# Key norms of a random-feature attention computed by two-column products and applied as the bias of the exponential

## The chip, the cores and the metric

The kernel runs on one core of a Trainium2 chip. The metric is the device time of one execution, in microseconds (us); lower is better. The kernel before took 1992.07 us in the median of three runs (1990.9 to 1998.57).

## The reference, cut to what matters

The program is two layers of a graph network on 625 nodes with 768 channels: normalisation, a graph convolution and an attention side by side, then a feed-forward part (the second one a mixture of experts). The change touches only the second layer's attention. It has 12 heads of 64 channels and 256 random features, and is linear in the number of nodes:

```
def _phi(t, random_features):
    norm_sq = 0.5 * jnp.sum(t * t, axis=-1, keepdims=True)
    proj = jnp.einsum('bhnd,md->bhnm', t, random_features)
    return jnp.exp(proj - norm_sq) * (1.0 / math.sqrt(M))
q_p = _phi(q, random_features)
k_p = _phi(k, random_features)
kv = jnp.einsum('bhnm,bhnd->bhmd', k_p, v)
out = jnp.einsum('bhnm,bhmd->bhnd', q_p, kv)
k_sum = jnp.sum(k_p, axis=2)
normalizer = jnp.einsum('bhnm,bhm->bhn', q_p, k_sum)[..., None]
out = out / (normalizer + 1e-06)
```

So each key row of each head needs one number, half the sum of its squares, which is subtracted from 256 projections before the exponential.

## The kernel before, in words

Every operand of a product is held as a high part (fp32r) and a low part (the rest), and a product is two or three matmuls of such parts. A high part is written by ScalarE (`ACT`), the low part by VectorE (`DVE`) as a difference.

The attention is the function `phase_attend`, which is used twice; the second time with `second` true, between 1000 and 1172 us of the profiled execution. After the values it runs over six pairs of heads (`for p in range(PAIRS)`). Each engine has its own queue, written out by hand, and they meet by semaphores. On TensorE one pair is:

- `features_k(p)`: five key tiles of up to 128 nodes. For each tile two products with 512 columns put minus half the squared norm into all 512 columns of a PSUM bank (line 407: the weights are the squares `sq`, the moving operand is `nh`, which holds -0.5 in the rows of one head and 0 in those of the other), and four products with 256 columns add the projections of the two heads (line 411). The banks are 6 and 7 by turns. Between the tiles stand units of the next pair's projection to queries and keys (`project_unit`, six products each, line 191).
- `features_q(p)`: four query tiles (two heads by two halves of the features) of eight products with 314 columns (lines 437 and 445), with a unit of projection after each of the first three.
- `keys_values(p)`: 40 products with 130 columns (line 464), then three more units of projection.
- `attend(p)`: 24 products (line 191) that give numerators and denominators of both heads.

On ScalarE each key tile is two exponentials of all 512 columns from PSUM: line 580 writes the full value to the scratch `pf`, line 581 the high part to `phik`. Then come the next pair's keys (`qk_high`, line 532), the query tiles with two exponentials each (lines 597 and 598) and, after the first of them, the squares of the next keys (`squares`, lines 544 and 545), a piece of the weight ring (`ring_high`, line 128), the high part of the key-value matrix (lines 609 and 613), the next pair's queries, the denominators (line 626), and the squares of the next queries. The second squares go to `sqf`, from which GpSimd makes the low part of the squares (line 346).

On VectorE each key tile is the low part (line 721). After each of the first four key tiles stands the reciprocal of a quarter of the previous pair's denominators (line 729). Then come the next keys' low part (line 681), `normalise(p - 1)` (line 690, numerators times reciprocals), the low parts of the four query tiles (line 742), a piece of the weight ring (line 139), the key-value matrix (lines 759, 762 and 767), the next queries' low part and a copy of the numerators (line 783). The scratch `pf` has two buffers, so an exponential waits for the low part two tiles earlier.

Of the kernel before, what the change touches and what calls it, by code (L numbers as in the profile page):

```python
# [258 lines left out]
def phase_attend(k, name, second, rf=None):  # L259
# [3 lines left out]
    with ExitStack() as ctx:  # L263
# [15 lines left out]
        if second:  # L279
            scratch = k.x[:].rearrange("p t d -> p (t d)")  # L280
            pf = scratch[:, 0:2 * NT].rearrange("p (a n) -> p a n", a=2)
            sqf = scratch[:, 2 * NT:4 * NT].rearrange("p (a n) -> p a n", a=2)
            den = scratch[:, 4 * NT:5 * NT]
            sq = k.sb(f"{name}_sq", [P, 2, 2, NT], F32R)
            nh = k.sb(f"{name}_nh", [P, 512], F32R)
            tiny = k.sb(f"{name}_tiny", [P, 1], F32)
            k.x_dram = k.nc.dram_tensor("x_dram", (NODES, D), F32).ap()
        else:
            bv, bq, bp = k.v_bias, k.qk_bias, k.out_bias
        s = signals(k, name, (  # L290
            "saved", "rf_in", "chain", "ones_set", "rf_turned", "rf_bd", "rf_hi", "rf_ready", "v_mm", "v_f", "v_hi",
            "v_lo", "qk_mm", "qk_hi", "qk_lo", "sq_hi", "sq_lo", "pk_mm", "pk_f", "pk_hi", "pk_lo",
            "pq_mm", "pq_f", "pq_hi", "pq_lo", "kv_mm", "kv_part", "kv_f", "kv_hi", "kv_lo", "at_mm", "den_f", "num_f",
            "at_out"))
# [8 lines left out]
        def qk_count(p, a):  # L303
            return 2 * p + (1 if a == KEYS else 2)

        def key_bank(t):
            return k.banks[6 + t % 2][0:TS[t], 0:512]

        def query_pair(m):
            return k.pair[0] if m % 2 == 0 else k.pair[3]  # L310
# [43 lines left out]
        def _(pe):  # L354
# [20 lines left out]
            def project_unit(p, u):  # L375
# [13 lines left out]
                if j == KD - 1:  # L389
                    mm.then_inc(s["qk_mm"], 1)  # L390

            def features_k(p):
                pe.wait_ge(s["qk_lo"], qk_count(p, KEYS))
                for t in range(TT):
                    i = p * TT + t
                    if i >= 2:
                        pe.wait_ge(s["pk_hi"] if second else s["pk_lo"], i - 1)
                    if t < 2 and p >= 1:
                        pe.wait_ge(s["pq_hi"] if second else s["pq_lo"], 4 * p)
                        if second:  # L400
                            pe.wait_ge(s["den_f"], 2 * p - 1)
                            pe.wait_ge(s["num_f"], 2 * p - 1)
                    if second:
                        if t == 0:
                            pe.wait_ge(s["sq_lo"], qk_count(p, KEYS))
                        for a in range(2):
                            pe.matmul(key_bank(t), sq[:, KEYS, a, t * P:t * P + TS[t]], nh[:], start=(a == 0), stop=False)
                    for hd in range(2):
                        out = key_bank(t)[:, hd * MF:(hd + 1) * MF]
                        for a in range(2):  # L410
                            mm = pe.matmul(out, qk[:, KEYS, hd, t * P:t * P + TS[t]], rf2[:, a, :],
                                           start=(a == 0 and not second), stop=(a == 1 and (hd == 1 or not second)))
                    mm.then_inc(s["pk_mm"], 1)
                    project_unit(p + 1, t)
                project_unit(p + 1, TT)
# [91 lines left out]
        def _(act):  # L507
# [61 lines left out]
            for p in range(PAIRS):  # L569
                for t in range(TT):  # L570
                    i = p * TT + t
                    act.wait_ge(s["pk_mm"], i + 1)
                    if p >= 1 and t == 0:
                        act.wait_ge(s["kv_mm"], p)
                    if second:
                        if t >= 2:
                            act.wait_ge(s["pk_lo"], i - 1)
                        elif p >= 1:
                            act.wait_ge(s["pq_lo"], 4 * p)
                        act.activation(pf[0:TS[t], t % 2, 0:512], key_bank(t), FUNC).then_inc(s["pk_f"], 1)  # L580
                    act.activation(phik[0:TS[t], t, 0, :], key_bank(t), FUNC).then_inc(s["pk_hi"], 1)
                    if not second and p >= 1 and t in (1, 2):
                        qk_high(p, QUERIES, (t - 1,))
                if p + 1 < PAIRS:
                    qk_high(p + 1, KEYS, (0, 1) if second else (0,))
                for m in range(4):
                    i = p * 4 + m
                    src = query_pair(m)[:, :, 0:HN]
                    act.wait_ge(s["pq_mm"], i + 1)
                    if p >= 1 and m == 0:  # L590
                        act.wait_ge(s["at_mm"], 2 * p)
                    if second:
                        if m >= 2:
                            act.wait_ge(s["pq_lo"], i - 1)
                        else:
                            act.wait_ge(s["pk_lo"], TT * (p + 1))
                        act.activation(halves(pf[:, m % 2, :]), src, FUNC).then_inc(s["pq_f"], 1)
                    act.activation(halves(phiq[:, m, 0, :]), src, FUNC).then_inc(s["pq_hi"], 1)
                    if m == 0 and p + 1 < PAIRS and not second:
                        qk_high(p + 1, KEYS, (1,))  # L600
                    if m == 0 and p + 1 < PAIRS and second:
                        squares(p + 1, KEYS)
                if p + 5 <= len(st.chunks):
                    ring_high(act, st, p + 5)
                act.wait_ge(s["kv_mm"], p + 1)
                if p >= 1:
                    act.wait_ge(s["kv_f"], p)
                for hd in range(2):
                    ins = act.activation(kvt[:, 2 * hd:2 * hd + 2, :], kv_bank(hd)[:, :, DH + 2:VW], ACT.Copy, scale=KV_SCALE)
                ins.then_inc(s["kv_part"], 1)  # L610
                act.wait_ge(s["kv_f"], p + 1)
                if second:
                    ins = act.activation(kv[:, 0, :, :], kvf[:], ACT.Copy)
                else:
                    for hd in range(2):
                        ms = slice(2 * hd, 2 * hd + 2)
                        ins = act.activation(kv[:, 0, ms, own(hd)], kvf[:, ms, own(hd)], ACT.Copy)
                ins.then_inc(s["kv_hi"], 1)
                if p + 1 < PAIRS and second:
                    qk_high(p + 1, QUERIES)  # L620
                if second:
                    if p >= 1:
                        act.wait_ge(s["at_out"], p)
                    for n, hd in enumerate((1, 0)):
                        act.wait_ge(s["at_mm"], 2 * p + n + 1)
                        act.activation(halves(den[own(hd), :]), num_pair(hd)[other(hd), :, 0:HN], ACT.Identity,
                                       bias=tiny[other(hd), 0:1]).then_inc(s["den_f"], 1)
                    if p + 1 < PAIRS:
                        squares(p + 1, QUERIES)
                else:  # L630
                    for n, hd in enumerate((1, 0)):
                        act.wait_ge(s["at_mm"], 2 * p + n + 1)
                        act.activation(halves(at_f[own(hd), p, :]), num_pair(hd)[other(hd), :, 0:HN], ACT.Copy)\
                            .then_inc(s["at_out"], 1)

        @block.vector
        def _(dve):
# [37 lines left out]
            def qk_low(p, a, heads=(0, 1)):  # L675
                for hd in heads:
# [8 lines left out]
                    if hd == 1:  # L685
                        ins.then_inc(s["qk_lo"], 1)

            def normalise(p):
                dve.wait_ge(s["num_f"], 2 * p + 2)
                dve.tensor_tensor(at_f[:, p, :], at_f[:, p, :], den, ALU.mult).then_inc(s["at_out"], 1)  # L690
# [22 lines left out]
            else:  # L713
                ring_low(dve, st, 4)
                values(2)
            for p in range(PAIRS):
                for t in range(TT):
                    dve.wait_ge(s["pk_hi"], p * TT + t + 1)
                    hi = phik[0:TS[t], t, 0, :].bitcast(F32)
# [2 lines left out]
                    else:  # L722
                        ins = dve.scalar_tensor_tensor(phik[0:TS[t], t, 1, :], key_bank(t), 0.0, hi, ALU.max, ALU.subtract)
                    ins.then_inc(s["pk_lo"], 1)
                    if second and p >= 1 and t < 4:
                        quarter = den[:, t * (NT // 4):(t + 1) * (NT // 4)]
                        if t == 0:
                            dve.wait_ge(s["den_f"], 2 * p)
                        ins = dve.reciprocal(quarter, quarter)
                        if t == 3:  # L730
                            link(ins)
                    if not second and p >= 1 and t in (1, 2):
                        qk_low(p, QUERIES, (t - 1,))
                if p + 1 < PAIRS:
                    qk_low(p + 1, KEYS, (0, 1) if second else (0,))
                if second and p >= 1:
                    normalise(p - 1)
                for m in range(4):
                    dve.wait_ge(s["pq_hi"], p * 4 + m + 1)
                    hi = phiq[:, m, 0, :].bitcast(F32)  # L740
                    if second:
# [3384 lines left out]
```

## Time and profile before

| | us |
|---|---|
| median of three runs | 1992.07 |
| the profiled execution | 1992.17 |
| its span, first to last instruction | 1990.4 |
| TensorE busy (PE) | 1898.1 |
| VectorE busy (DVE) | 1209.1 |
| ScalarE busy (ACT) | 860.3 |
| GpSimd busy (POOL) | 86.9 |

PE is TensorE's matmuls and PEld its weight loads, which overlap them. A duration in the profile is that of one instruction from its start to its end; two instructions that follow each other on an engine can overlap by a little, so their spacing is less than a duration. PEclk is the clock that TensorE was granted, 1.00 for 2.4 GHz and 0.50 for 1.2 GHz. A timeline row gives start, duration (of all merged instructions, from the first start to the last end), engine, line, operation, output and inputs, count, and in brackets how long the engine sat idle before it and what released it.

### The profile page before, as it was taken

To read this page: it belongs to the slowest core of one execution; us is meant where nothing else is said; L and a number is where in the kernel's file an instruction comes from. 1 tells how busy PE (TensorE), PEld (TensorE's weight loads), DVE (VectorE), ACT (ScalarE), POOL (GpSimd) and SP (SyncE) were. 2 spreads that over 40 slices of the span, in tenths; PEclk is the share of its full clock that TensorE was granted. 3 is DMA by queue.
4 is the path that set the end of the run, shared out by engine and by line. 5 is a ranking of instruction groups with operands and counts; after the bars stand their busy time and mean duration, and the time that the engine had idled before them with its cause. 6 is when DMAs were issued, how large, how long until landed. Compare 5 with 4: busy or idle time off the path is not lost. (4 is left out here: it accounts for less than half of the span.)

```text
span 1990.4 us, 32417 instructions
## 1 busy us (share of the span) xinstructions
PE 1898.1 (95%) x13147; PEld 1789.1 (90%) x13147; DVE 1209.1 (61%) x1898; ACT 860.3 (43%) x1138; POOL 86.9 (4%) x80
## 2 busy tenths in 40 slices
PE   5899899999999999999999989799999999999999
PEld 4899789999999999998899989698878888888899
DVE  8566687444343345446566667765666668998732
ACT  6445522222212212224466652423565557777620
POOL 0000000000000000000010000000111001100000
PEclk9999999999999999999999999899999999999999
DMA  3311036111111113110211041423977679999831
GB/s 91 97 33 49 27 84 176 56 56 56 56 56 57 51 37 92 49 49 17 88 33 33 17 135 57 158 76 109 330 230 235 211 233 319 370 372 379 303 119 39
DMA packets 157963, 250.54 MB, mean 126 GB/s; under 512 B 11949, under 2 KB 86189, under 8 KB 157460
## 3 DMA queue, kind: packets, MB, share of 16 engines
q1 hardware_dynamic: 152532, 231.21, 34.9%
q0 software_dynamic: 5040, 17.56, 3.6%
q8 instruction: 90, 1.47, 0.3%
q14 instruction: 29, 0.24, 0.0%
q10 hardware_dynamic: 272, 0.07, 0.0%
HBM read 228.80 MB, written 20.01 MB: 125 GB/s over the span
## 5 line engine op out<-in xcount | busy, mean ns | idle before, releaser
L183 PE MATMUL psum<-products_room 128*128 128x512 f32 (+2 forms) x2160 | 457.2, 366 | 3.1 <-DVE re_credit L3605 2.0
L183 PEld LDWEIGHTS psum<-products_room 128*128 128x128 f32 (+1 forms) x2160 | 388.4, 187 | 47.1 <-issue 2.3
L183 PE MATMUL psum<-ring_hi,xt_sb 128*128 128x256 f32 (+3 forms) x1920 | 354.6, 283 | 9.5 <-PEq L1183 2.8
L3502 DVE TENSOR_TENSOR products_room<-moe_raw,products_room 128x1536 fp32r<-128x1536 f32 x179 | 312.5, 1755 | 77.3 <-ACT products_room L3401 76.9
L3401 ACT ACTIVATE products_room<-moe_raw 128x1536 fp32r<-128x1536 f32 x179 | 265.9, 1489 | 152.0 <-PE psum L183 82.5
L183 PEld LDWEIGHTS psum<-ring_hi,xt_sb 128*128 128x128 f32 (+1 forms) x1920 | 299.3, 188 | 11.2 <-issue 6.1
L183 PE MATMUL psum<-ring_lo,xt_sb 128*128 128x256 f32 (+3 forms) x960 | 270.4, 282 | 0.0
L183 PEld LDWEIGHTS psum<-ring_lo,xt_sb 128*128 128x128 f32 (+1 forms) x960 | 180.3, 188 | 0.0
L183 PE MATMUL psum<-ring_hi,gnn_sb 128*128 128x256 f32 (+1 forms) x810 | 150.0, 286 | 5.4 <-DVE gnn_sb L1086 3.6
L139 DVE TENSOR_TENSOR ring_lo<-ring_raw,ring_hi 128x1536 fp32r<-128x1536 f32 (+1 forms) x64 | 119.4, 1866 | 54.1 <-ACT ring_hi L128 54.0
L191 PE MATMUL psum<-xt_sb,ring_hi 128*128 128x314 f32 x744 | 139.2, 309 | 0.3
L128 ACT ACTIVATE ring_hi<-ring_raw 128x1536 fp32r<-128x1536 f32 (+1 forms) x65 | 101.9, 1568 | 81.6 <-PE psum L191 32.2
L183 PEld LDWEIGHTS psum<-ring_hi,gnn_sb 128*128 128x128 f32 (+1 forms) x810 | 127.3, 191 | 6.3 <-issue 4.3
L191 PE MATMUL psum<-xt_sb,products_room 128*128 128x314 f32 x864 | 127.3, 309 | 2.1 <-DVE products_room L3945 1.1
L191 PEld LDWEIGHTS psum<-xt_sb,products_room 128*128 128x128 f32 x864 | 126.0, 189 | 2.8 <-issue 1.4
L1600 ACT ACTIVATE g_y<-psum 128x256 fp32r<-128x256 f32 (+3 forms) x100 | 37.8, 379 | 198.5 <-PE psum L1533 103.9
L1649 DVE TENSOR_TENSOR g_y<-psum,g_y 128x256 fp32r<-128x256 f32 (+3 forms) x100 | 41.5, 417 | 134.2 <-ACT g_y L1600 134.0
L1554 PE MATMUL psum<-gnn_sb,g_y 128*128 128x314 f32 (+1 forms) x780 | 117.2, 308 | 0.0
L183 PE MATMUL psum<-ring_lo,gnn_sb 128*128 128x256 f32 (+1 forms) x405 | 115.6, 286 | 0.0
L191 PEld LDWEIGHTS psum<-xt_sb,ring_hi 128*128 128x128 f32 x744 | 114.6, 189 | 1.0 <-issue 1.0
L1554 PEld LDWEIGHTS psum<-gnn_sb,g_y 128*128 128x128 f32 (+1 forms) x780 | 114.3, 190 | 0.2 <-DVE g_cnt L1625 0.2
L191 PE MATMUL psum<-xt_sb,ring_lo 128*128 128x314 f32 x372 | 84.5, 308 | 0.0
(517 smaller groups left out, 2772.1 us busy)
## 6 DMA issues: line engine op xcount, KB each, us to landing
moe_raw<-in_L_ffn_Wg_r SPq DMA_DIRECT2D x60, 768.0 KB, 6.1
moe_raw<-in_L_ffn_Wu_r SPq DMA_DIRECT2D x60, 768.0 KB, 6.1
moe_raw<-in_L_ffn_Wd_r SPq DMA_DIRECT2D x60, 768.0 KB, 8.7
ring_raw<-in_L_gnn_w_rel SPq DMA_DIRECT2D x18, 896.0 KB, 5.0
ring_raw<-in_L_mix_W_qkv SPq DMA_DIRECT2D x24, 384.0 KB, 4.2
ring_raw<-in_L_gnn_w_rel SPq DMA_DIRECT2D x9, 768.0 KB, 4.5
ring_raw<-in_L_gnn_w_root SPq DMA_DIRECT2D x6, 896.0 KB, 5.1
count_total_dram<-gnn_sb POOLq DMA_DIRECT2D x3, 1570.0 KB, 12.2
```

Source lines behind the costliest of these rows:

```text
L128: act.activation(ring.hi[:, g % RING_SLOTS, 0:size], ring.raw[:, g % RING_SLOTS, 0:size], ACT.Copy).then_inc(ring.hi_done, 1)
L139: dve.tensor_tensor(lo, raw, hi.bitcast(F32), ALU.subtract).then_inc(ring.lo_done, 1)
L183: mm = pe.matmul(out, lhs[a], rhs[b], start=(first and i == 0), stop=(last and i == 2))
L191: mm = pe.matmul(bank_pair[:, h, 0:HN], lhs[a], rhs(b, h), start=(first and i == 0), stop=(last and i == 2))
L1554: mm = pe.matmul(pair[:, h, 0:HN], y[0:TS[t], v % 2, t, a, col + m * P:col + (m + 1) * P], k.C[0:TS[t], r, t, h * HN:(h + 1) * HN], start= ...
L1600: act.activation(y[0:TS[t], v % 2, t, 0, 0:w], k.banks[i % 3][0:TS[t], 0:w], ACT.Copy).then_inc(s["y_hi"], 1)
L1649: dve.tensor_tensor(y[0:TS[t], v % 2, t, 1, 0:w], k.banks[i % 3][0:TS[t], 0:w], y[0:TS[t], v % 2, t, 0, 0:w].bitcast(F32), ALU.subtract).t ...
L3401: act.activation(whi[:, slot, :], raw[i % RAWS], ACT.Copy).then_inc(s["hi_done"], 1)
L3502: dve.tensor_tensor(wlo[:, i % RING, :], raw[i % RAWS], whi[:, i % RING, :].bitcast(F32), ALU.subtract)\
```

## The change

The norms of the keys no longer go through the bank of the projections. `key_norms(p)` stands ahead of the key tiles: for each of the five tiles two products whose moving operand is only two columns of `nh` (one per head) put the negative half norms of both heads into two columns of bank 7. VectorE copies the ten columns to the new tile `key_norm` in two copies. ScalarE makes the exponential of a key tile in two halves of 256 columns, one per head, with the column of `key_norm` as bias, into `pf`; it then waits for its own result and copies `pf` to `phik` for the high part. TensorE now waits for `pf` (`pk_f`) rather than for `phik` before it writes a key bank again. On VectorE the first two quarters of the reciprocal stand after key tiles 0 and 2, the last two and `normalise` after the second query tile.

```
@@ phase_attend: tiles, signals, banks
+            key_norm = k.sb(f"{name}_key_norm", [P, 2 * TT], F32)
-            "saved", "rf_in", "chain", "ones_set", "rf_turned", "rf_bd", "rf_hi", "rf_ready", "v_mm", "v_f", "v_hi",
+            "saved", "rf_in", "chain", "ones_set", "rf_turned", "rf_bd", "rf_hi", "rf_ready", "kn_mm", "kn_f", "v_mm", "v_f", "v_hi",
+        def norm_bank():
+            return k.banks[7]
@@ tensor
+            def key_norms(p):
+                pe.wait_ge(s["sq_lo"], qk_count(p, KEYS))
+                if p >= 1:
+                    pe.wait_ge(s["pk_f"], TT * p)
+                    pe.wait_ge(s["pq_hi"], 4 * p)
+                    pe.wait_ge(s["den_f"], 2 * p - 1)
+                    pe.wait_ge(s["num_f"], 2 * p - 1)
+                for t in range(TT):
+                    for a in range(2):
+                        mm = pe.matmul(norm_bank()[0:TS[t], 2 * t:2 * t + 2], sq[:, KEYS, a, t * P:t * P + TS[t]],
+                                       nh[:, MF - 1:MF + 1], start=(a == 0), stop=(a == 1))
+                mm.then_inc(s["kn_mm"], 1)
+
             def features_k(p):
+                if second:
+                    key_norms(p)
                 pe.wait_ge(s["qk_lo"], qk_count(p, KEYS))
                 for t in range(TT):
                     i = p * TT + t
                     if i >= 2:
-                        pe.wait_ge(s["pk_hi"] if second else s["pk_lo"], i - 1)
-                    if t < 2 and p >= 1:
-                        pe.wait_ge(s["pq_hi"] if second else s["pq_lo"], 4 * p)
-                        if second:
-                            pe.wait_ge(s["den_f"], 2 * p - 1)
-                            pe.wait_ge(s["num_f"], 2 * p - 1)
-                    if second:
-                        if t == 0:
-                            pe.wait_ge(s["sq_lo"], qk_count(p, KEYS))
-                        for a in range(2):
-                            pe.matmul(key_bank(t), sq[:, KEYS, a, t * P:t * P + TS[t]], nh[:], start=(a == 0), stop=False)
+                        pe.wait_ge(s["pk_f"] if second else s["pk_lo"], i - 1)
+                    if t < 2 and p >= 1 and not second:
+                        pe.wait_ge(s["pq_lo"], 4 * p)
+                    if second and t == 1:
+                        pe.wait_ge(s["kn_f"], p + 1)
@@ scalar, key tile
-                        act.activation(pf[0:TS[t], t % 2, 0:512], key_bank(t), FUNC).then_inc(s["pk_f"], 1)
-                    act.activation(phik[0:TS[t], t, 0, :], key_bank(t), FUNC).then_inc(s["pk_hi"], 1)
+                        if t == 0:
+                            act.wait_ge(s["kn_f"], p + 1)
+                        for hd in range(2):
+                            half = slice(hd * MF, (hd + 1) * MF)
+                            ins = act.activation(pf[0:TS[t], t % 2, half], key_bank(t)[:, half], FUNC,
+                                                 bias=key_norm[0:TS[t], 2 * t + hd:2 * t + hd + 1])
+                        ins.then_inc(s["pk_f"], 1)
+                        act.wait_ge(s["pk_f"], i + 1)
+                        act.activation(phik[0:TS[t], t, 0, :], pf[0:TS[t], t % 2, 0:512], ACT.Copy).then_inc(s["pk_hi"], 1)
@@ vector
             for p in range(PAIRS):
+                if second:
+                    dve.wait_ge(s["kn_mm"], p + 1)
+                    if p >= 1:
+                        dve.wait_ge(s["pk_f"], TT * p)
+                    dve.tensor_copy(key_norm[:, 0:2 * TT - 2], norm_bank()[:, 0:2 * TT - 2])
+                    dve.tensor_copy(key_norm[0:TS[TT - 1], 2 * TT - 2:2 * TT], norm_bank()[0:TS[TT - 1], 2 * TT - 2:2 * TT])\
+                        .then_inc(s["kn_f"], 1)
...
-                    if second and p >= 1 and t < 4:
-                        quarter = den[:, t * (NT // 4):(t + 1) * (NT // 4)]
+                    if second and p >= 1 and t in (0, 2):
                         if t == 0:
                             dve.wait_ge(s["den_f"], 2 * p)
-                        ins = dve.reciprocal(quarter, quarter)
-                        if t == 3:
-                            link(ins)
+                        invert(t // 2)
...
-                if second and p >= 1:
-                    normalise(p - 1)
                 for m in range(4):
+                    if second and p >= 1 and m == 2:
+                        invert(2)
+                        link(invert(3))
+                        normalise(p - 1)
                     dve.wait_ge(s["pq_hi"], p * 4 + m + 1)
```

## Rows read from the trace of the kernel before

**Rows 1.** The page's busy times of the engines over the whole span.
```profile
PE 1898.1 (95%) x13147; PEld 1789.1 (90%) x13147; DVE 1209.1 (61%) x1898; ACT 860.3 (43%) x1138; POOL 86.9 (4%) x80
```

**Rows 2.** Windows: us, then busy us by engine, granted clock; pair 2, and inside pair 5.
```profile
1057.18:1085.38 28.20, 28.02 (x200) 27.29 (x199) 20.10 (x26) 19.61 (x32) 3.08 (x2) 1.00 0.11 29
...
1162.00:1167.00 5.00, 2.94 (x11) 2.94 (x12) 1.31 (x5) 0.63 (x1) 0.00 (x0) 0.58 0.00 0
```

**Rows 3.** Timeline of TensorE's matmuls in pair 2.
```profile
1058.98 0.63 PE L407 MATMUL psum<-m_nh,m_sq 128*128 128x512 f32 x2
...
1059.45 0.63 PE L411 MATMUL psum<-m_rf,m_qk 128*128 128x256 f32 x4
...
1059.92 0.74 PE L191 MATMUL psum<-xt_sb,ring_hi 128*128 128x314 f32 x4
...
1060.80 0.63 PE L407 MATMUL psum<-m_nh,m_sq 128*128 128x512 f32 x2
...
1073.22 0.74 PE L437 MATMUL psum<-m_qk,m_rf 128*128 128x314 f32 x4
...
1074.38 4.58 PE L464 MATMUL psum<-m_v,m_phik 128*128 128x130 f32 x40
1078.79 0.80 PE L191 MATMUL psum<-xt_sb,ring_hi 128*128 128x314 f32 x4
...
1081.80 3.75 PE L191 MATMUL psum<-m_phiq,m_kv 128*128 128x314 f32 x24 [0.17 <-DVE m_kv L767]
```

**Rows 4.** Timeline of ScalarE in pair 2.
```profile
1059.35 0.60 ACT L580 ACTIVATE x_sb<-psum 128x512 f32<-128x512 f32 x1
1059.83 0.62 ACT L581 ACTIVATE m_phik<-psum 128x512 fp32r<-128x512 f32 x1
...
1067.30 1.41 ACT L532 ACTIVATE m_qk<-psum 64x628 fp32r<-64x628 f32 x2 [0.66 <-PE psum L191]
...
1071.68 0.71 ACT L598 ACTIVATE m_phiq<-psum 128x628 fp32r<-128x628 f32 x1
```

**Rows 5.** Timeline of VectorE in pair 2.
```profile
1063.16 1.12 DVE L729 RECIPROCAL x_sb<-x_sb 128x157 f32<-128x157 f32 x1
...
1064.20 0.63 DVE L721 TENSOR_TENSOR m_phik<-x_sb,m_phik 128x512 fp32r<-128x512 f32 x1
...
1069.87 0.81 DVE L690 TENSOR_TENSOR a_sb<-a_sb,x_sb 128x628 f32<-128x628 f32 x1
1070.60 0.81 DVE L742 TENSOR_TENSOR m_phiq<-x_sb,m_phiq 128x628 fp32r<-128x628 f32 x1
...
1072.42 1.08 DVE L742 TENSOR_TENSOR m_phiq<-x_sb,m_phiq 128x628 fp32r<-128x628 f32 x1 [1.01 <-ACT m_phiq L598]
...
1077.40 1.76 DVE L139 TENSOR_TENSOR ring_lo<-ring_raw,ring_hi 128x1536 fp32r<-128x1536 f32 x1 [0.70 <-ACT ring_hi L128]
...
1079.47 0.29 DVE L759 SCALAR_TENSOR_TENSOR m_kvf<-psum,m_kvt 128x128 f32<-128x128 f32 x1 [0.31 <-ACT m_kvt L609]
```

**Rows 6.** Groups by line and shape, for prices: busy us and mean ns of one.
```profile
L2528 ACT ACTIVATE p_graph<-psum,dinv 128x256 fp32r<-128x256 f32 x12 | 5.6, 469 | 7.7 <-PE psum L183 7.7
...
L613 ACT ACTIVATE m_kv<-m_kvf 128x512 fp32r<-128x512 f32 x6 | 3.8, 631 | 5.7 <-DVE m_kvf L762 5.7
...
L3109 DVE CAST products_room<-a_sb 128x28 fp32r<-128x28 f32 x10 | 1.8, 179 | 0.0
...
L895 PE MATMUL psum<-count_over,ones_r 128*128 128x2 f32 x1 | 0.2, 166 | 0.0
```

**Rows 7.** Timeline of the last pair: its start, its last key tile, its attend.
```profile
1141.80 0.64 PE L407 MATMUL psum<-m_nh,m_sq 128*128 128x512 f32 x2
...
1152.08 0.69 DVE L721 TENSOR_TENSOR m_phik<-x_sb,m_phik 113x512 fp32r<-113x512 f32 x1
...
1152.88 0.69 ACT L597 ACTIVATE x_sb<-psum 128x628 f32<-128x628 f32 x1 [2.29 <-DVE m_phik L721]
...
1164.06 6.23 PE L191 MATMUL psum<-m_phiq,m_kv 128*128 128x314 f32 x24 [2.84 <-DVE m_kv L767]
```

More of the change, by code:

```diff
@@ L411, in features_k @@
                             mm = pe.matmul(out, qk[:, KEYS, hd, t * P:t * P + TS[t]], rf2[:, a, :],
-                                           start=(a == 0 and not second), stop=(a == 1 and (hd == 1 or not second)))
+                                           start=(a == 0), stop=(a == 1))
                     mm.then_inc(s["pk_mm"], 1)
@@ L579, in _ @@
                             act.wait_ge(s["pq_lo"], 4 * p)
-                        act.activation(pf[0:TS[t], t % 2, 0:512], key_bank(t), FUNC).then_inc(s["pk_f"], 1)
-                    act.activation(phik[0:TS[t], t, 0, :], key_bank(t), FUNC).then_inc(s["pk_hi"], 1)
+                        if t == 0:
[7 more added lines that the diff above has]
+                        act.activation(phik[0:TS[t], t, 0, :], pf[0:TS[t], t % 2, 0:512], ACT.Copy).then_inc(s["pk_hi"], 1)
+                    else:
+                        act.activation(phik[0:TS[t], t, 0, :], key_bank(t), FUNC).then_inc(s["pk_hi"], 1)
                     if not second and p >= 1 and t in (1, 2):
@@ L686, in qk_low, with invert @@
                         ins.then_inc(s["qk_lo"], 1)
+            def invert(q):
+                quarter = den[:, q * (NT // 4):(q + 1) * (NT // 4)]
+                return dve.reciprocal(quarter, quarter)
             def normalise(p):
```

## The prediction, written before the changed kernel was run

> **What bounds the kernel now.** I read the page's busy times first: TensorE is busy for 95% of the span [rows 1], so time is to be had only where TensorE has less to do, and only as long as nothing else then ends last. Next the windows of the second attention. In pair 2 TensorE is busy for 28.02 of 28.20 us at full clock, VectorE for 20.10, ScalarE for 19.61 [rows 2]. The timeline shows the same pattern in the first five of the six pairs, so there TensorE is the bound, with VectorE and ScalarE some 8 us behind. The reader is to see two more things. The only stall of TensorE in such a pair is 0.17 us ahead of attend, for the key-value matrix from VectorE [rows 3]; what VectorE does ahead of that matrix has only 0.31 us of slack, the idle time ahead of line 759 [rows 5]. And the last pair is of another kind: it has no projection units, its first query exponential waits 2.29 us for VectorE's last key tile, and TensorE waits 2.84 us ahead of attend and then runs it in 6.23 us instead of 3.75, the granted clock being 0.58 in that stretch [rows 2, 7].
>
> I count from T, the start of a pair's key tiles (1057.18 in pair 2, 1141.80 in the last).
>
> **TensorE, part by part.** Removed: two 512-column products in each of five tiles. Line 407 starts at 1058.98 and line 411 at 1059.45, so two cost 0.47 us, five tiles 2.35 us [rows 3]. Added: ten products of two columns, each with its own load of 128 columns of weights. The trace has no row of such products with their spacing. From above: 40 products of 130 columns with a weight load each take from 1074.38 to 1078.79, 0.110 us each [rows 3]; the one two-column product in the trace lasts 0.166 us [rows 6], and no overlap at all would make that the spacing. From below I halve the 0.110, the share of 128 weight columns in 258 columns passed, as an estimate: 0.055. I take 0.110, since the weight load is the same one: 1.10 us a pair. So TensorE gains 2.35 - 1.10 = 1.25 us a pair; the ends are 0.69 and 1.80.
>
> The Trainium skill (TensorE: Matmul & The Clock Gate, section Back-to-back issue gap) puts products of 128 columns with their weight loads 81 ns apart, against the 110 of this trace for 130 columns. By it the ten would take 0.81 us and only the first pair would gain 0.29 us more, since the others are held by what follows.
>
> **The new wait for the norms.** They are in bank 7 at T+1.10; VectorE's two copies cost about 0.18 us each (the nearest row is a cast of 28 columns, 179 ns [rows 6]), so the bias is there at T+1.5. VectorE has nothing due behind them before the first key tile is done. TensorE wants bank 7 at T+2.45 (1.10 + 0.47 + 0.88 for a unit, the 0.88 from 1059.92 to 1060.80 [rows 3]), ScalarE starts its first tile at T+2.17 (1059.35 [rows 4]), where the denominators and squares ahead of it in its queue put it. Hidden, with 0.67 us to spare. No DMA is added or moved.
>
> **ScalarE.** Before, a tile is two exponentials 0.48 us apart with 0.60 duration, so neighbours overlap by 0.12 [rows 4], 0.96 us in all. Now: two halves of 256 columns with an operand per partition. The nearest row is line 2528, 128x256 from PSUM with a scale per partition, 0.47 us [rows 6]. The second half starts at 0.35 and ends at 0.82; the wait for its own result costs 0.03, as between line 598's end (1072.39) and line 742's start (1072.42) [rows 4, 5]; the copy from SBUF is the form of line 613, 0.63 us [rows 6]. So a tile's high part is ready after 1.48 us, and the next tile starts after 0.85 + 0.63 - 0.12 = 1.36 us. Ends: without any overlap 0.47 + 0.47 + 0.03 + 0.63 + 0.03 = 1.63, with each half at half of the old 0.60, 0.30, it would be 0.18 + 0.30 + 0.03 + 0.51 = 1.02. Five tiles from T+2.17: the next instruction, line 532, could start at T+8.97. It needs TensorE's sixth unit, which it had at T+10.12 [rows 4] and now has at T+8.87. So ScalarE, not TensorE, sets it, and everything after it on ScalarE is 1.15 us earlier than before. TensorE's tiles (1.35 us each) need the exponential two tiles back: the third, at T+3.80, needs T+2.17+0.82; no wait there, since that wait now ends with `pf` and not with the copy.
>
> The Trainium skill (ScalarE: Activation LUTs, section What ACT_TABLE_LOAD costs) gives 280 ns + 0.833 ns a column with a bias operand, 186 + 0.833 without, and 93 ns of overlap. By it a tile is 0.89 + 0.03 + 0.52 = 1.44 us. The five tiles end 0.4 us later, and the sum below would be 1987.5.
>
> **VectorE.** In the key stage it loses two reciprocals (spacing 1.04 us, 1063.16 to 1064.20 [rows 5]); its low parts keep up with 1.36 us a tile: for tile 1 it is ready at T+5.5, and ScalarE asks for that at T+6.25. What was moved stands later in the same queue, and here is the tight place. The low part of query tile 1 started at T+15.24 (1072.42), now T+14.09, and ends 1.08 us later [rows 5]. Then: first reciprocal at T+15.09, second at 16.13, done at 17.25, its wait 17.28, normalise 0.73 (the spacing 1069.87 to 1070.60 [rows 5]) to 18.01, low parts of query tiles 2 and 3 to 19.47, the ring's low part 1.76 [rows 5] to T+21.23. Only then can line 759 start. It started at T+22.29, and TensorE and ScalarE would now allow 22.29 - 1.25 = T+21.04. So VectorE ends last there by 0.19 us, and attend, which hangs on the key-value matrix, is 1.06 us earlier, not 1.25. Query tile 3 on TensorE (1073.22, T+16.04 [rows 3], new 14.79) needs query tile 1's high part at T+14.09: 0.7 us to spare.
>
> **The sum.** Pair 0 has no reciprocals: 1.25 us. Pairs 1 to 4: 4 x 1.06 = 4.24. Pair 5: the last key tile starts at T+2.17+4x1.36 = 7.61, its high part is there at 9.09, its low part (0.69 [rows 7]) at 9.81, and the first query exponential 0.11 us later as before, T+9.92 instead of T+11.08: 1.16 us, and the chain behind it keeps its length (the moved reciprocals lie beside the 40 products of line 464). Together 6.65 us. The profiled execution took 1992.17 us around a span of 1990.4, 0.1 above the median of the runs: 1992.17 - 6.65 = 1985.5 us.
>
> **Rivals.**
> (a) VectorE is not late (the reciprocals or the copies overlap more than I have it): 6 x 1.25 = 7.5, 1984.7 us. For it: my lateness is only 0.19 us. Against it: each of five durations stands in a row.
> (b) The two-column products cost 0.166 each: TensorE gains 0.69 a pair, and VectorE, ready at T+21.23, is no longer asked before T+21.60: 5 x 0.69 + 1.16 = 4.6, 1987.6 us. For it: the duration in rows 6. Against it: the 130-column products are 0.110 apart although one lasts 4.58 - 39 x 0.110 = 0.29.
> (c) The clock in the last pair. TensorE's work in its key stage is thinner than before: ten products of two columns, then four of 256 with waits for ScalarE between. The drop to 1.2 GHz that now falls on attend, at a price of 6.23 - 3.75 = 2.5 us, may come elsewhere or twice: 2.5 us better, 1983.0, or, with the query and key-value products also at half speed for about 3 us of work, 3 us worse, 1988.5. For it: rows 7 show that the pair sits at the edge. Against it: much of the key stage would hide a slow TensorE behind ScalarE.
> (d) Slower than before: the ScalarE tile without overlap, 1.63 us, the halves and the copy waiting for each other. Each of the five tiles is then 0.27 us later, 1.35 in all, VectorE reaches line 759 at T+22.58, 0.29 later than before: pairs 1 to 4 lose 1.2 us together. In pair 0 query tile 3 then waits 0.65 us on TensorE, which leaves 0.6 of its gain, and pair 5 stays as it was (first query exponential at T+11.12): 1992.17 + 1.2 - 0.6 = 1992.8 us. It decides from a tile of 1.57 us on, where the 1.06 us are used up. For it: the added wait of ScalarE for itself. Against it: the overlap of neighbours in rows 4.
>
> **Chances.** The forecast 0.50, (a) 0.12, (b) 0.12, (c) 0.16, (d) 0.10. The range 1982.0 to 1990.0 holds (a) to (c) and leaves out (d) and what lies beyond either end of (c). A measurement of this kernel can tell about 0.5%, 10 us, from no change. For faster by that (below 1982) the clock must help and the products be at their lower price: 0.10. Slower by that (above 2002) would need (d) and a stall that I don't see: 0.05. Within 0.5%: 0.85.
>
> **What would show it.** Right: the key stage's first product to the next pair's, 27.1 to 27.2 us instead of 28.20; ten products in 1.1 us; key tiles on ScalarE 1.36 us apart; line 759's successor waiting for VectorE's own queue and not for ScalarE; the wait ahead of attend about 0.36 instead of 0.17 us. Wrong: a spacing of the ScalarE tiles of 1.5 us or more, stalls of TensorE between key tiles of the first five pairs, a period of 28 us, or a last pair that is longer than before at half clock.

## The result and the profile after

The changed kernel took 1987.14 us in the median of twelve runs (1984.05 to 1996.89), the kernel before, beside it, 1995.22 (1990.9 to 2004.63): a ratio of 0.9966 with a 95% interval of 0.995 to 0.9981, which is 6.8 us (3.8 to 10) less. That is clear of no change, though smaller than the scatter of single runs. The profiled execution of the changed kernel took 1984.05 us around a span of 1982.3.

The windows of pair 2 and of the last pair's attend in the changed kernel (they answer to [rows 2]; there the second window also held some waiting):

```profile
1053.28:1080.69 27.41, 26.84 (x200) 26.57 (x199) 19.80 (x28) 20.94 (x37) 3.10 (x2) 1.00 0.10 30
...
1156.90:1162.00 5.10, 5.04 (x24) 4.78 (x24) 0.82 (x1) 0.78 (x1) 0.00 (x0) 0.71 0.00 0
```

Pair 2 is 27.41 us long instead of 28.20, and TensorE, the bound before, now sits idle for 0.57 us of it instead of 0.18. The timeline of TensorE in pair 2 shows where (these answer to [rows 3]):

```profile
1053.28 1.15 PE L405 MATMUL psum<-m_nh,m_sq 128*128 128x2 f32 x10
1054.29 0.72 PE L424 MATMUL psum<-m_rf,m_qk 128*128 128x256 f32 x4
...
1055.71 0.63 PE L424 MATMUL psum<-m_rf,m_qk 128*128 128x256 f32 x4
...
1057.06 0.64 PE L424 MATMUL psum<-m_rf,m_qk 128*128 128x256 f32 x4
...
1069.28 4.58 PE L477 MATMUL psum<-m_v,m_phik 128*128 128x130 f32 x40
...
1077.10 3.76 PE L191 MATMUL psum<-m_phiq,m_kv 128*128 128x314 f32 x24 [0.57 <-DVE m_kv L799]
```

Ten two-column products take 1.01 us, the tiles are 1.35 us apart, only the first is 1.42, and line 477 (464 before) starts at T+16.00 instead of T+17.20: TensorE gained 1.20 us. Attend starts only 0.80 us earlier (T+23.82, before T+24.62). Where the other 0.40 us went is in ScalarE's and VectorE's timelines (they answer to [rows 4, 5]):

```profile
1054.88 0.69 ACT L558 ACTIVATE m_sq<-psum 128x628 fp32r<-128x628 f32 x1
1055.59 0.84 ACT L597 ACTIVATE x_sb<-psum,m_key_norm 128x256 f32<-128x256 f32 x2
1056.46 0.63 ACT L601 ACTIVATE m_phik<-x_sb 128x512 fp32r<-128x512 f32 x1
1057.00 0.82 ACT L597 ACTIVATE x_sb<-psum,m_key_norm 128x256 f32<-128x256 f32 x2
...
1062.57 1.39 ACT L545 ACTIVATE m_qk<-psum 64x628 fp32r<-64x628 f32 x2
```
```profile
1067.64 1.09 DVE L774 TENSOR_TENSOR m_phiq<-x_sb,m_phiq 128x628 fp32r<-128x628 f32 x1 [1.53 <-ACT m_phiq L620]
1068.65 2.12 DVE L712 RECIPROCAL x_sb<-x_sb 128x157 f32<-128x157 f32 x2
1070.81 0.81 DVE L716 TENSOR_TENSOR a_sb<-a_sb,x_sb 128x628 f32<-128x628 f32 x1
1071.54 1.53 DVE L774 TENSOR_TENSOR m_phiq<-x_sb,m_phiq 128x628 fp32r<-128x628 f32 x2
1072.98 1.75 DVE L139 TENSOR_TENSOR ring_lo<-ring_raw,ring_hi 128x1536 fp32r<-128x1536 f32 x1
1074.77 0.29 DVE L791 SCALAR_TENSOR_TENSOR m_kvf<-psum,m_kvt 128x128 f32<-128x128 f32 x1
```

ScalarE's tiles are 1.40 us apart, and its next instruction (line 545) starts at T+9.29. VectorE works from 1067.64 to 1074.77 with no idle time that the profile names, and line 791 has no bracket: it waited for nothing but its own queue. In the last pair (start at T = 1135.53) the first query exponential starts at T+10.22 and attend at T+21.40; this row answers to [rows 7]:

```profile
1156.93 5.04 PE L191 MATMUL psum<-m_phiq,m_kv 128*128 128x314 f32 x24 [2.84 <-DVE m_kv L799]
```

The stage, from its first key product to the end of the last attend, took 169.5 us before and 163.2 after, 6.3 less: 1.06 in pair 0, 4 x 0.79 in pairs 1 to 4, 0.86 in the last pair up to attend, and 1.19 in attend itself. That last term is clock: attend's window shows a granted clock of 0.71, and the same 24 products before the change had 0.55:

```profile
1164.06:1170.29 6.23, 6.23 (x24) 5.97 (x24) 0.82 (x1) 0.78 (x1) 0.00 (x0) 0.55 0.00 0
```

The span became 8.1 us shorter; 2.0 of that lie ahead of the stage, where the two kernels do the same. They are clock too: the kernel before loses 3.0 us in two stretches in which it was granted less, and wins back 1.0 elsewhere. The two stretches, before and then after:

```profile
920.00:930.00 10.00, 7.62 (x40) 6.90 (x41) 4.99 (x17) 5.70 (x12) 0.00 (x0) 0.83 0.01 2
952.00:967.00 15.00, 13.23 (x99) 13.10 (x100) 7.08 (x23) 5.88 (x14) 0.00 (x0) 0.89 0.04 13
```
```profile
920.00:930.00 10.00, 7.56 (x50) 6.87 (x49) 6.40 (x20) 6.77 (x12) 0.00 (x0) 1.00 0.01 2
952.00:967.00 15.00, 13.12 (x110) 12.80 (x111) 8.43 (x28) 6.61 (x16) 0.00 (x0) 1.00 0.18 63
```

### The profile page after: what moved, and what is told of

Same layout as the page of the kernel before. It is cut to its first block and busy times, and to the rows that moved or that the text cites. A ratio compares the mean times of both kernels' runs of the same rounds, so it can differ in the third digit from the quotient of the medians.

```text
span 1982.3 us, 32465 instructions
## 1 busy us (share of the span) xinstructions
PE 1888.4 (95%) x13147; PEld 1782.9 (90%) x13147; DVE 1207.9 (61%) x1910; ACT 869.1 (44%) x1168; POOL 86.6 (4%) x80
```

## The experiments

One table holds what was read from the timelines of all, in us: the period (from a pair's T to the next one's) of pair 0 and of pairs 1 to 4, the start of the last pair's attend after its T, and the duration of the whole stage. Each line is one profiled execution. `norms twice`, `no bias` and `four halves` ran only that once, so for them there is no ratio of times. The last two columns hold the clock of the last pair too, which differed from profile to profile.

| kernel | pair 0 | pairs 1 to 4 | last attend at | stage |
|---|---|---|---|---|
| before | 28.20 | 28.2 | 22.26 | 169.5 |
| changed | 27.14 | 27.41 | 21.40 | 163.2 |
| norms alone | 27.15 | 27.62 | 22.38 | 166.2 |
| move alone | 28.23 | 28.23 (once 28.36) | 20.22 | 166.8 |
| norms twice | 28.24 | 28.14 (twice 29.65) | 21.99 | 170.8 |
| three and one | 27.15 | 27.02 | 21.42 | 162.7 |
| mixed | 27.03 | 27.02 | 20.22 | 160.3 |
| no bias | 27.04 | 27.05 | 21.51 | 162.7 |
| four halves | 27.95 | 27.71 | 22.28 | 166.3 |

**The norms alone.** The reciprocals and `normalise` back in their old places:

```
-                    if second and p >= 1 and t in (0, 2):
+                    if second and p >= 1 and t < 4:
...
-                        invert(t // 2)
+                        ins = invert(t)
+                        if t == 3:
+                            link(ins)
...
+                if second and p >= 1:
+                    normalise(p - 1)
                 for m in range(4):
-                    if second and p >= 1 and m == 2:
-                        invert(2)
-                        link(invert(3))
-                        normalise(p - 1)
```

> The two-column norms alone; the four reciprocals and normalise stand where they stood in the kernel before. Theory (VectorE's queue is what holds pairs 1 to 4 and the last pair): the key stage of VectorE is then 0.57 + 1.04 = 1.6 us a tile against 1.4 of ScalarE, the fifth low part ends at about T+11.1, the squares of the next keys and query tile 1 on ScalarE are 0.5 to 0.9 us later than in the changed kernel; the period of pairs 1 to 4 is 27.7 us (27.41 in the changed kernel, 28.20 before), and the last pair's attend starts 0.9 us later than in the changed kernel, no earlier than in the one before. In all 3 us faster than before. Rival (TensorE's 1.2 us is all that counts and the move only a detail): period 27.4 as in the changed kernel.

Measured: 0.9971 of the kernel before (0.9955 to 0.9987), which is 5.8 us (2.6 to 9.0) less where 3 were expected; the stage is 3.3 us shorter. Period 27.62, and the last attend at T+22.38, no earlier than before. VectorE's key stage in pair 2 (T = 1060.20):

```profile
1066.25 1.13 DVE L712 RECIPROCAL x_sb<-x_sb 128x157 f32<-128x157 f32 x1
1067.29 0.63 DVE L754 TENSOR_TENSOR m_phik<-x_sb,m_phik 128x512 fp32r<-128x512 f32 x1
1067.83 1.13 DVE L712 RECIPROCAL x_sb<-x_sb 128x157 f32<-128x157 f32 x1
1068.87 0.63 DVE L754 TENSOR_TENSOR m_phik<-x_sb,m_phik 128x512 fp32r<-128x512 f32 x1
...
1070.58 0.69 DVE L754 TENSOR_TENSOR m_phik<-x_sb,m_phik 113x512 fp32r<-113x512 f32 x1
```

The low parts are about 1.6 us apart, VectorE has no idle time, and the fifth ends at T+11.07. ScalarE waits 0.52 us for that one, and by way of the query tiles it reaches TensorE, which stands still ahead of its last query tile:

```profile
1075.54 0.84 PE L450 MATMUL psum<-m_qk,m_rf 128*128 128x314 f32 x4 [0.33 <-ACT m_phiq L620]
```

So without the move the last pair gains nothing from the norms, and pairs 1 to 4 gain 0.58 instead of 0.79.

**The move alone.** The kernel before with `invert(2)`, `invert(3)` and `normalise` behind query tile 1 (cut; `normalise` is taken out of its old place):

```
-                    if second and p >= 1 and t < 4:
+                    if second and p >= 1 and t in (0, 2):
...
                 for m in range(4):
+                    if second and p >= 1 and m == 2:
+                        invert(2)
+                        link(invert(3))
+                        normalise(p - 1)
```

> The kernel before with the second half of the reciprocals and normalise moved behind query tile 1; norms as before. Theory: in pairs 1 to 4 the moved work reaches line 759's successor 0.1 us after it is asked for, period 28.2 to 28.3 us (28.20 before); in the last pair, where VectorE's key tiles hold everything, the first query exponential starts at about T+9.1 instead of T+11.08, attend 2.0 us earlier. In all 1.5 us faster than before. Rival (the move costs VectorE its slack): period 28.8 or more. Rival (the last pair is gained by the norms, not by the move): attend of the last pair as before, T+22.3.

Measured: 0.9987 (0.9971 to 1.0002), which the times can't tell from no change; the timeline can. The pairs keep their 28.23 us and the last attend starts at T+20.22, 2.04 earlier. In the changed kernel it starts at T+21.40. So on top of the move the norms cost 1.18 us in the last pair, and its gain of 0.86 is what they leave of the move's 2.04: with no projection units to hide behind, ScalarE's tile of 1.40 us is on the path. The two don't simply add up: without the move the norms cost 0.12 there (T+22.38 against T+22.26), since VectorE's reciprocals held the tiles anyway, and on top of the norms the move gives 0.98.

**The norms twice.**

```
-                for t in range(TT):
+                for t in [t for _ in range(2) for t in range(TT)]:
```

> The changed kernel with its ten two-column products done twice, the same result written again. Theory: TensorE has 1.00 us more a pair, of which VectorE's lateness ahead of attend (0.57 us idle against 0.17 before) takes 0.4, so the period of pairs 1 to 4 goes from 27.41 to about 28.0 and the idle time ahead of attend to 0.2; pair 0, where VectorE isn't late, takes the full 1.0 us. Rival (TensorE is the only bound): 28.4. Rival (VectorE alone sets the pair): 27.4.

Measured: the second ten products added 1.09 us on TensorE. Pair 0 took 1.10 us more, pairs 1 and 3 0.73 more, with 0.22 us idle ahead of attend. So in the changed kernel TensorE has about 0.35 us to spare in pairs 1 to 4 and none in pair 0, as VectorE's lateness has it. Pairs 2 and 4 weren't expected: 29.65 us. Windows of pair 2 (us, busy by engine, granted clock) and its timeline:

```profile
1063.58:1066.50 2.92, 2.92 (x28) 2.92 (x27) 1.04 (x3) 2.12 (x4) 0.56 (x1) 1.00 0.00 0
1066.50:1070.00 3.50, 3.50 (x17) 3.50 (x16) 1.74 (x2) 2.78 (x6) 0.98 (x1) 0.52 0.00 0
```
```profile
1063.58 2.24 PE L405 MATMUL psum<-m_nh,m_sq 128*128 128x2 f32 x20
1065.68 0.72 PE L424 MATMUL psum<-m_rf,m_qk 128*128 128x256 f32 x4
...
1067.50 1.06 PE L424 MATMUL psum<-m_rf,m_qk 128*128 128x256 f32 x4
1068.36 1.25 PE L191 MATMUL psum<-xt_sb,ring_hi 128*128 128x314 f32 x4
```

The profile calls TensorE busy for all of the first window, in most of which it ran two-column products; the clock then fell from 2.4 to 1.2 GHz, and four products of 314 columns took 1.25 us instead of 0.74. It cost 1.5 us each time. In the nine other profiles the clock never fell in these five pairs (granted 1.00 over all of them), so the ten extra products are the likely cause; why it fell in two pairs and not in the other three, one execution doesn't show.

**Three reciprocals and one.** Three after key tiles 0, 1 and 2, the fourth with `normalise` behind query tile 0:

```
-                    if second and p >= 1 and t in (0, 2):
+                    if second and p >= 1 and t < 3:
...
-                    if second and p >= 1 and m == 2:
-                        invert(2)
+                    if second and p >= 1 and m == 1:
                         link(invert(3))
                         normalise(p - 1)
```

> The changed kernel with three reciprocals after key tiles 0, 1 and 2 and the last one with normalise between query tiles 0 and 1, into 1.5 us in which VectorE sits idle in the changed kernel. Theory: the key-value matrix is no longer late, the idle time ahead of attend goes from 0.57 to about 0.2 and the period of pairs 1 to 4 from 27.41 to 27.0; the last pair within 0.1 us of the changed kernel's; 1.5 us less in all than the changed kernel, which with its runs' scatter can't be told by the time alone, only in the periods. Rival (something else, ScalarE's chain, holds attend): period stays 27.4. Rival (three reciprocals in the key stage make VectorE late for ScalarE's scratch): period above 27.5.

Measured: 0.9962 (0.9946 to 0.9979), period 27.02. Line 790 of this kernel, the first of the key-value matrix, in pair 2 (T = 1057.45):

```profile
1078.55 0.29 DVE L790 SCALAR_TENSOR_TENSOR m_kvf<-psum,m_kvt 128x128 f32<-128x128 f32 x1 [0.41 <-ACT m_kvt L631]
```

It starts at T+21.10 and waits for ScalarE again; TensorE's wait ahead of attend is 0.18 us. So a change of nothing but the order of VectorE's queue gave the 0.39 us back in each of pairs 1 to 4. The last pair came as expected up to attend (T+21.42), but attend then took 6.04 us instead of 5.04, which is why the stage is only 0.5 us shorter than the changed kernel's.

**No bias.** `bias=key_norm[...]` is left out of the two halves, so the keys' half norms are missing from the result.

> The changed kernel, its halves of the key exponential with no bias operand (the norms are computed and waited for, but not applied: the keys' half norms are left out of the result). Theory (ScalarE's tile sets the key stage and, through VectorE's queue, attend): a half lasts 0.38 instead of 0.47 us, the second starts 0.26 after the first, the tile goes from 1.40 to about 1.21 us, TensorE's units then hold ScalarE's tiles at 1.35, VectorE reaches the key-value matrix 0.3 us or more earlier and the period of pairs 1 to 4 goes to 27.1; the last pair's attend, where nothing but ScalarE holds the key tiles, to T+20.6. Rival (the operand costs latency only): the tile stays at 1.4 and nothing moves.

Measured: half exponentials of 0.38 us, and tiles 1.21 us apart where nothing else holds them (pair 3, T = 1090.12):

```profile
1092.29 0.67 ACT L597 ACTIVATE x_sb<-psum 128x256 f32<-128x256 f32 x2
1092.99 0.63 ACT L600 ACTIVATE m_phik<-x_sb 128x512 fp32r<-128x512 f32 x1
1093.53 0.64 ACT L597 ACTIVATE x_sb<-psum 128x256 f32<-128x256 f32 x2
1094.20 0.63 ACT L600 ACTIVATE m_phik<-x_sb 128x512 fp32r<-128x512 f32 x1
1094.74 0.64 ACT L597 ACTIVATE x_sb<-psum 128x256 f32<-128x256 f32 x2
```

The first of them starts at T+2.17, as before the change; with a bias it starts at T+2.31, after the end of the squares ahead of it (1054.88 + 0.69). So the operand costs 0.19 us a tile and 0.14 once, and the period goes to 27.05 as expected (27.1). The last pair did not follow: attend at T+21.51 instead of T+20.6. In that pair the clock fell:

```profile
1144.23:1150.10 5.87, 4.30 (x32) 3.68 (x31) 3.37 (x6) 5.54 (x12) 1.53 (x1) 1.00 0.00 0
1150.10:1156.90 6.80, 6.23 (x25) 5.79 (x24) 4.02 (x7) 5.08 (x11) 0.00 (x0) 0.50 0.01 4
```

ScalarE's first query exponential starts at T+9.50, 0.72 us earlier than in the changed kernel, but what it gave the query products at 1.2 GHz took back: eight of them took 2.1 us instead of 1.2, and ScalarE's second query tile waits for them:

```profile
1155.44 0.69 ACT L618 ACTIVATE x_sb<-psum 128x628 f32<-128x628 f32 x1 [0.43 <-PE psum L458]
```

**Four halves.** The high part by two more half exponentials from PSUM, in place of ScalarE's wait for itself and the copy:

```
-                        act.wait_ge(s["pk_f"], i + 1)
-                        act.activation(phik[0:TS[t], t, 0, :], pf[0:TS[t], t % 2, 0:512], ACT.Copy).then_inc(s["pk_hi"], 1)
+                        for hd in range(2):
+                            half = slice(hd * MF, (hd + 1) * MF)
+                            ins = act.activation(phik[0:TS[t], t, 0, half], key_bank(t)[:, half], FUNC,
+                                                 bias=key_norm[0:TS[t], 2 * t + hd:2 * t + hd + 1])
+                        ins.then_inc(s["pk_hi"], 1)
```

(and TensorE waits for `pk_hi` before it writes a key bank again).

> The changed kernel with the high part made by two more half exponentials from PSUM with bias instead of the wait for its own result and the copy from SBUF. Theory: four halves 0.36 apart are 1.45 to 1.5 us a tile against 1.40, so ScalarE's chain is 0.3 to 0.5 us later at the end of the key stage and the period of pairs 1 to 4 is 27.7 to 27.9. Rival (the wait for its own result is the expensive part): the tile below 1.35 and the period 27.2 or less.

Measured: tiles 1.43 us apart, a little less than expected, and period 27.71, at the low end of what was expected. The copy behind a wait is the cheaper form by 0.03 us a tile on ScalarE. That is 0.15 of the 0.30 us that the period grew; the rest comes behind the key tiles, where the next activations start later too. In pair 0, 0.81 us longer than the changed kernel's, the other part of the edit shows, which the expectation left out: TensorE now waits for the high part before it writes a bank again:

```profile
1005.05 0.74 PE L424 MATMUL psum<-m_rf,m_qk 128*128 128x256 f32 x4 [0.47 <-ACT m_phik L602]
```

**Mixed.** `three and one` for pairs 1 to 4; the last pair's keys as before the change, with its reciprocals moved; and an early exponential for the table load, which in the changed kernel stood behind the wait for the norms of pair 0 (cut; TensorE's waits and VectorE's part are left out):

```
+                lone = second and p == PAIRS - 1
+                if second and not lone:
+                    key_norms(p)
...
+            if second:
+                act.activation(warm[:], k.one[:], FUNC)
...
+                        if p == PAIRS - 1:
+                            act.activation(pf[0:TS[t], t % 2, 0:512], key_bank(t), FUNC).then_inc(s["pk_f"], 1)
+                            act.activation(phik[0:TS[t], t, 0, :], key_bank(t), FUNC).then_inc(s["pk_hi"], 1)
+                            continue
```

> The changed kernel with (1) three reciprocals in the key stage and the fourth with normalise between query tiles 0 and 1, in pairs 1 to 4; (2) the last pair's keys as in the kernel before (512-column norm products, two whole exponentials from PSUM), with the reciprocals moved behind its second query tile; (3) one small exponential ahead of pair 0, so that the table load doesn't wait for the norms. Theory, from the periods measured so far: pair 0 27.0 to 27.1 us, pairs 1 to 4 27.0 each, last pair's attend at T+20.2 instead of T+21.40. Against the changed kernel 4 x 0.4 + 1.2 = 2.8 us less, against the kernel before 1.1 + 4 x 1.2 + 2.0 = 7.9 us, a ratio of 0.996 (0.9945 to 0.9975 with what the clock scatters). Rival (the last pair's gain is lost to the clock again): attend starts at T+20.2 but takes over 6 us instead of 5.04 in the changed kernel's profile.

Measured: 0.9949 (0.9929 to 0.9969), median 1986.66 us beside 1995.41. Every period and the last attend (T+20.22, then 5.03 us) came as expected; the stage is 9.2 us shorter than before, 8.0 by the queues and 1.2 by the clock in attend.

**The changed kernel again**, beside the mixed one:

> The changed kernel once more, on the same chip and beside the same runs of the kernel before. Theory: periods 27.1 and 4 x 27.4, attend of the last pair at T+21.4; ratio 0.995 to 0.998; about 2.8 us slower than the mixed kernel, which is at the edge of what five rounds can tell. Where the granted clock falls in the last pair differs from profile to profile.

Measured: 0.9972 (0.9954 to 0.9991), with periods 27.16 and 27.4 and the last attend at T+21.41. The mixed kernel's ratio is 0.0023 lower, 4.6 us where 2.8 were expected; the two intervals overlap, so that the mixed kernel is the faster one is shown by the stage (160.3 and 163.4 us in their profiles) and only likely by the times.

This profile also shows one source of the kernel's scatter. Two profiles of the same kernel, the first and this one, in a stretch of the first layer that no kernel here changes:

```profile
225.00:260.00 35.00, 26.96 (x175) 25.39 (x174) 22.85 (x40) 16.90 (x28) 0.81 (x2) 0.85 0.30 90
```
```profile
225.00:260.00 35.00, 27.36 (x133) 25.46 (x132) 18.40 (x32) 15.41 (x25) 0.80 (x2) 0.61 0.19 60
```

At a clock of 0.61 instead of 0.85 it got through 133 products instead of 175. The second attention began at 1009.53 us instead of 998.73, and 5.9 us of these 10.8 arise in this stretch (the same activation near its start is 0.7 us late, that of line 1000 near its end 6.6). The clock goes with the scatter of the twelve runs in the result too: the three above 1994 us had a mean granted clock of 0.979, the fastest 0.989, the others 0.980 to 0.987. They spread over 13 us, more than any effect tested here.

## Why the prediction came out right, and where its terms were off

The forecast was 6.65 us less, the measured ratio says 6.8 (3.8 to 10). The mechanism held: TensorE's relief, cut short by VectorE's queue. Four terms had the wrong size, and the clock added to the total.

- **TensorE, 1.25 us a pair: 1.20.** The ten products took 1.01 us, nearer to my 1.10 than to either end; the first key tile behind them is 0.07 longer. Rival (b), 0.166 each, is out.
- **VectorE late ahead of the key-value matrix, gain 1.06 in pairs 1 to 4: 0.79.** The chain was the predicted one, link by link (two reciprocals 2.12 us, no gap up to line 791), and `three and one` removed it. It began 0.27 us later than I had it, at T+14.36, because ScalarE left the key tiles 0.32 later (T+9.29, not T+8.97): its first tile started 0.14 later, since a half with a bias did not overlap the squares ahead of it, and five tile spacings were 1.40 instead of 1.36. By an estimate from the Trainium skill (ScalarE: Activation LUTs, section What ACT_TABLE_LOAD costs) the tile would be 1.44; the trace lies between that and mine. Rival (a) is out, and (d) too: its tile would be 1.63. One reading was loose: VectorE's low part of key tile 1, said to be ready at T+5.5, started then and ended at T+6.13. Nothing hung on it, as ScalarE asked for it at T+6.50.
- **Pair 0, 1.25: 1.06.** "Hidden, with 0.67 us to spare" failed there: it was worked out for a pair with another one ahead of it. The exponential's table load stood behind the new wait. ScalarE's timeline in pair 0 of the changed kernel (T = 998.73):

```profile
998.92 0.39 ACT L533 ACTIVATE m_v<-psum 113x256 fp32r<-113x256 f32 x1 [1.74 <-PE psum L183]
1000.22 1.28 ACT L597 ACT_TABLE_LOAD   x1 [0.91 <-DVE m_key_norm L748]
1001.51 0.84 ACT L597 ACTIVATE x_sb<-psum,m_key_norm 128x256 f32<-128x256 f32 x2
```

It waits 0.91 us for the norms' copy, then loads, and the first tile starts at T+2.78. Loading it early gave 0.11 us back in the mixed kernel, whose gain of 1.17 in pair 0 is about TensorE's own 1.20. In `no bias` the load stands where it stood and pair 0 took 27.04 us as well, so the late start costs something only together with the tile of 1.40.
- **The last pair, 1.16: 0.86.** I had seen it as one gain. The shortfall of 0.30 is ScalarE again: the first tile 0.14 later and four spacings 0.04 longer, so that the first query exponential starts at T+10.22 and not T+9.92. The two experiments take the gain apart: the move alone gives 2.04, and the norms on top of it cost 1.18. That the norms cost time there at all stood nowhere in my sum.
- **The clock, rival (c).** It decided more than I gave it. In the first profile it added 1.2 us in attend and 2.0 ahead of the stage to the 5.1 us that the queues gave. The whole 2.5 us that (c) hoped for never came: TensorE sat idle for 2.84 us ahead of the last attend in all ten profiles, and attend took 4.99 to 6.23 us in them, never the 3.75 of full clock. The second drop did come: in the last pair's key or query products the clock fell in five of the seven profiles with the two-column norms there (not in the first one of the changed kernel and not in `norms alone`), and in none of the three with the old form. Twice it cost nothing up to attend, because ScalarE hid it (the changed kernel again T+21.41, `three and one` T+21.42); in `no bias` it ate 0.9 us. So that the total came out at 6.65 is partly luck: the queues gave 5.1, which the interval holds as well.

Was it the clock that made the changed kernel faster? The record answers in part. Its 24 runs had a mean granted clock of 0.983, the 46 of the kernel before whose clock is on record 0.982. Over all runs with a clock on record, each kernel taken by itself, 0.01 of clock goes with 8.0 us. By that estimate the clock's share in the difference of the means, 6.7 us, is 0.7, and 6.0 us (give or take 1) are left at equal clock: nearer to the queues' 5.1 than the profiled execution's 8.1. What makes up the other 0.9 is not shown.

## What to carry to other kernels

A product got through 512 moving columns in 0.235 us here, 130 in 0.110 and 2 in 0.10, each with its own load of 128 columns of weights: nearly all of the gain lies above 130 columns, and a product of a few columns still costs 0.10 us. When TensorE is the bound, count what its relief asks of the other queues stage by stage: 1.2 us less on TensorE gave 0.8, because work moved within VectorE's queue stood ahead of the next thing asked for, and a place with 1.5 us idle was one query tile earlier. A stage without the filler work of the others (a first or a last iteration) can lose by a change from which the others gain; here the old form in the last pair and the new one elsewhere was the best of the kernels tried (stage 160.3 us).

## What the runs showed of the hardware

- TensorE at 100% busy in the profile lost its clock: after 20 products of two columns in 2.1 us it went from 2.4 to 1.2 GHz in two of the first five pairs (it stayed up in the other three, and in all five in the nine profiles without the extra products), and four products of 314 columns went from 0.74 to 1.25 us.
- A half exponential (128x256 from PSUM) takes 0.46 us with a bias per partition and 0.38 without; the first one with a bias started only at the end of the activation ahead of it (0.71 us after its start), one without 0.58 after.
- A table load takes its place behind a wait that stands ahead of the first exponential: 0.91 us of waiting, then 1.28 us of loading.
